# The last layer's experts: first products with their outputs on lanes, norm weight and mean folded into the second weights

## The reference, cut to what matters

```
scores = xf @ gate_w + gate_b            # expert 0 masked out, softmax, top 3
h = gelu(einsum('td,edh->eth', xf, fc1_w) + fc1_b)        # 16 experts, width 384
mu, var = h.mean(-1), h.var(-1)
h = (h - mu) * rsqrt(var + 1e-5) * ln_w[e] + ln_b[e]      # a norm inside each expert
y = einsum('eth,ehd->etd', h, fc2_w) + fc2_b
out = einsum('te,etd->td', combine, y)
```

## Time and profile before

| | us |
|---|---|
| median of 3 runs | 1077.01 (1073.15 to 1079.69) |
| profiled execution, its own time | 1074.89 |
| span of the profile | 1073.1 |
| mean granted clock | 0.876 |

### The profile page before, as it was taken

The page is one execution under the profiler, slowest core; times in us unless marked ns, Lnnn a source line. Parts: engine busy times, 40 slices in busy tenths (PEclk is TensorE's granted clock), DMA queues, the critical chain, the costliest instruction groups (busy, mean ns, idle before and its releaser), DMA issues. The chain is left out here.

```text
span 1073.1 us, 18222 instructions
## 1 busy us (share of the span) xinstructions
PE 897.4 (84%) x5969; PEld 710.9 (66%) x5969; DVE 441.0 (41%) x1153; ACT 307.6 (29%) x647; POOL 334.1 (31%) x373
## 2 busy tenths in 40 slices
PE   6887999787888887998888999998895386778684
PEld 4565899474576557777576999997665365556462
DVE  1234222322152158999482222221417926444342
ACT  2221122223344135443310222221332230323321
POOL 0002455000003218885013444443000001656650
PEclk9977899798769999999899999999986585879886
DMA  9215699100000042220043889998400004746653
GB/s 371 80 42 176 210 307 316 40 1 1 1 2 2 1 159 59 59 60 1 25 174 112 295 303 311 314 318 261 98 1 1 2 2 148 251 151 210 206 142 94
DMA packets 47378, 142.35 MB, mean 133 GB/s; under 512 B 6995, under 2 KB 11222, under 8 KB 47062
## 3 DMA queue, kind: packets, MB, share of 16 engines
q1 hardware_dynamic: 37846, 117.66, 32.3%
q0 software_dynamic: 9472, 23.93, 8.2%
HBM read 128.07 MB, written 13.50 MB: 132 GB/s over the span
## 5 line engine op out<-in xcount | busy, mean ns | idle before, releaser
L1168 POOL DMA_INDIRECT L_xr<-x_rows_L,L_rows_in x96 | 93.6, 975 | 42.2 <-issue 24.3
L1793 DVE TENSOR_TENSOR L_act<-L_hid,bank 116x512 f32<-116x512 f32 (+1 forms) x56 | 35.8, 640 | 155.8 <-ACT L_hid L1762 155.8
L1682 POOL DMA_INDIRECT y_rows_L<-L_yb,L_rows_out x56 | 55.7, 995 | 101.5 <-ACT L_yb L1768 94.9
L1762 ACT ACTIVATE L_hid<-bank 116x512 f32<-116x512 f32 (+1 forms) x56 | 31.3, 559 | 152.8 <-PE bank L1732 152.8
L1726 PE MATMUL bank<-L_xtb,L_w 128*116 128x128 f32 (+1 forms) x464 | 59.2, 282 | 0.0
L1070 POOL TENSOR_TENSOR ssm_w_low<-ssm_wbc,ssm_w_high 128x512 fp32r<-128x512 f32 x24 | 49.0, 2040 | 31.8 <-ACT ssm_w_high L1035 31.8
L1488 POOL COPY L_xrow<-L_xrow 96x384 f32<-96x384 f32 x3 | 1.5, 498 | 181.4 <-ACT L_xrow L1472 181.4
L1726 PEld LDWEIGHTS bank<-L_xtb,L_w 128*116 128x116 f32 (+1 forms) x464 | 56.6, 192 | 0.0
L1117 DVE TENSOR_TENSOR_SCAN ssm_state<-ssm_decay,ssm_drive 128x576 f32<-128x576 f32 x24 | 55.5, 2312 | 0.8
L228 PE MATMUL bank<-par_const 128*128 128x512 f32 x72 | 48.3, 800 | 0.8 <-issue 0.8
L987 PE MATMUL bank<-ssm_x_high,ssm_w_high 128*128 128x288 f32 x96 | 35.1, 365 | 13.0 <-DVE ssm_out L1122 8.8
(11 more groups left out here) (440 smaller groups left out, 2000.9 us busy)
## 6 DMA issues: line engine op xcount, KB each, us to landing
L_w<-in_L2w SPq DMA_DIRECT2D x20, 696.0 KB, 5.6
L_more<-in_L2w SPq DMA_DIRECT2D x20, 696.0 KB, 5.6
L_w<-in_L2w SPq DMA_DIRECT2D x20, 384.0 KB, 7.2
L_more<-in_L2w SPq DMA_DIRECT2D x20, 384.0 KB, 7.8
L_w<-in_L0w SPq DMA_DIRECT2D x12, 576.0 KB, 4.7
L_more<-in_L0w SPq DMA_DIRECT2D x12, 576.0 KB, 5.3
ssm_wbc<-in_wBC SPq DMA_DIRECT2D x24, 256.0 KB, 2.6
L_w<-in_L3w SPq DMA_DIRECT2D x16, 384.0 KB, 3.7
```

The lines of the kernel that those rows point to most:

```text
L1168: pool.indirect_dma_start(self.xr[j][:, :], None, self.x_rows[:, :], bass.IndirectOffsetOnAxis(ap=at, axis=0))\
L1682: pool.indirect_dma_start(X.y_rows[:, :], bass.IndirectOffsetOnAxis(ap=rows_out[h][:, j:j + 1], axis=0), y[s + j][:, :], None).then_inc(st ...
L1762: act.activation(hid[j][:, :, :], cols(gate_bank[j % 2][0:N, 0:C * R], C), ACT.Silu).then_inc(acted, 1)
L1793: dve.tensor_tensor(act_out[j][:, :, :], hid[j][:, :, :], cols(up_bank[j % 2][0:N, 0:C * R], C), ALU.mult)\
```

## The change

In the last layer's experts:

- The first product has the hidden features on the lanes (as in layers 0 and 2): 3 chunks x 2 halves, 128 tokens moving. Turning back and affine go.
- VectorE makes `centred = w2 * ln_w - shift[e]`, where `shift[e]` is the mean over the hidden features of `ln_w * w2`; this folds the norm's weight and the subtraction of the mean into the second weights. A column of ones gives the sum of the hidden values, and a one-column product with the squares their sum. The variance comes on VectorE, for two blocks at a time, its power -0.5 on GpSimd, and the output is scaled by gate x inverse deviation.
- `shift` comes from DRAM by a third load for each block, broadcast to 128 lanes. `ln_b @ w2` goes into the expert's bias (`fc2_b`).
- The steps overlap: a block's down product follows the next one's first product; SyncE loads the next step's weights after this step's first products; GpSimd's order is three gathers, the power of a pair, the fourth gather, two stores, the power of the second pair, two stores.
- Both sums over the experts' second weights, 16 x 3 products of 48 columns by 192, are made in the last attention: experts 0 to 8 between the scores and the first turned probabilities, 9 to 15 after them. There SyncE loads all second weights (288 KB each) and a selecting matrix (72 KB each), nine at a time, and ScalarE takes all scores before the first exponential.

```diff
--- head_attention
+            if also:
+                pe.wait_ge(sc_in, 7)
+                also.multiply(pe, T.bank[6], 0, 9)
             for g in range(BATCHES + 1):
                 if g < BATCHES:
                     turn(g)
+                if also and g == 0:
+                    also.multiply(pe, T.bank[6], 9, also.E)
                 if g:
                     apply(g - 1)
...
             scores(0)
             scores(1)
-            exponentials(0)
-            scores(2)
-            exponentials(1)
-            scores(3)
+            scores(2)
+            scores(3)
+            exponentials(0)
+            exponentials(1)
             take_turned(0)
             exponentials(2)
             take_turned(1)
+            also.keep_shifts(act, T.bank[6])
             add_bias(0)
...
+class SecondWeights:
+    def load(self, sp):
+        for e in range(self.E):
+            j = e % self.RING
+            if e >= self.RING:
+                sp.wait_ge(self.summed, e - self.RING + 1)
+            sp.dma_start(self.w[j][:, :], self.T.dram["L3w2"][e, :, 0:self.C * DIM]).then_inc(self.loaded[j], 16)
+            sp.dma_start(self.cols[j][:, :], self.T.dram["L3cols"][e, :, :]).then_inc(self.loaded[j], 16)
+        sp.wait_ge(self.shift_in, 1)
+        sp.dma_start(self.T.shifts, self.shift[32:48, :]).then_inc(self.stored, 16)
+        sp.wait_ge(self.stored, 16)
+    def multiply(self, pe, bank, first, end):
+        for e in range(first, end):
+            j = e % self.RING
+            pe.wait_ge(self.loaded[j], 32 * (e // self.RING) + 32)
+            for f in range(self.C):
+                mm = pe.matmul(bank[0:48, 0:DIM], self.cols[j][:, 48 * f:48 * f + 48], self.w[j][:, DIM * f:DIM * f + DIM],
+                               start=(e == 0 and f == 0), stop=(e == self.E - 1 and f == self.C - 1))
+            mm.then_inc(self.summed, 1)
...
--- run_normed_blocks, SyncE
                 for j in range(STEP):
-                    b = (q + 1) * STEP + j
-                    sp.wait_ge(down, b + 1)
-                    X.load(sp, b, STEP - s + j)
+                    sp.wait_ge(up, q * STEP + j + 1)
+                    X.load(sp, (q + 1) * STEP + j, STEP - s + j)
--- GpSimd
+                pool.tensor_copy(X.rows_in[1 - h][:, :], X.idx[:, bass.ds((q + 1) * STEP, STEP), 0]).then_inc(X.idx_in, 1)
+                pool.wait_ge(X.idx_in, q + 2)
+                fetch(0)
+                fetch(1)
+                fetch(2)
+                pool.wait_ge(stored[h], r * (16 * STEP) + 16)
+                pool.tensor_copy(rows_out[h][:, :], X.idx[:, bass.ds(q * STEP, STEP), 1]).then_inc(out_known, 1)
+                pool.wait_ge(out_known, q + 1)
+                invert(0)
+                fetch(3)
+                put(0)
+                put(1)
+                invert(1)
+                put(2)
+                put(3)
--- TensorE
+                def upwards(j):
+                    pe.wait_ge(xt_in, q * STEP + j + 1)
+                    pe.wait_ge(X.loaded[s + j], r * 48 + 48)
+                    if j >= 2:
+                        pe.wait_ge(acted, q * STEP + j - 1)
+                    for f in range(C):
+                        for c in range(2):
+                            at = I * c + N * f
+                            mm = pe.matmul(up_bank[j % 2][0:N, R * f:R * f + R], w1[s + j][:, at:at + N], xt[j][:, c, :],
+                                           start=(c == 0), stop=(c == 1))
+                    mm.then_inc(up, 1)
+                def downwards(j):
+                    pe.wait_ge(y_in, q * STEP + j + 1)
+                    pe.wait_ge(acted, q * STEP + j + 1)
+                    pe.wait_ge(weights_made, q * STEP + j + 1)
+                    for f in range(C):
+                        pe.matmul(down_bank[j][0:R, 0:DIM + 1], hid[j][:, f, :], centred[j][:, f, :],
+                                  start=(f == 0), stop=False)
+                    pe.wait_ge(squares_made, q * STEP + j + 1)
+                    for f in range(C):
+                        mm = pe.matmul(down_bank[j][0:R, DIM + 1:DIM + 2], square[j][:, f, :], p["ones"][:, 0:1],
+                                       start=False, stop=(f == C - 1))
+                    mm.then_inc(down, 1)
                 for j in range(STEP):
+                    if j + 1 < STEP:
+                        turn(pe, s + j + 1, r + 1, j + 1)
+                    upwards(j)
+                    if j:
+                        downwards(j - 1)
+                turn(pe, STEP - s, r + (2 if s else 1), STEP)
+                downwards(STEP - 1)
--- ScalarE (gelu: Gelu to hid, then Square; weigh: two outputs scaled by factor)
+                gelu(0)
+                take_gate(0)
+                take_gate(1)
+                gelu(1)
+                gelu(2)
+                take_gate(2)
+                take_gate(3)
+                gelu(3)
+                weigh(0)
+                weigh(1)
--- VectorE
+                def centre(j):
+                    dve.wait_ge(X.loaded[s + j], r * 48 + 48)
+                    dve.wait_ge(down, q * STEP + j + 1)
+                    for f in range(C):
+                        gain = C * DIM + f
+                        ins = dve.scalar_tensor_tensor(centred[j][:, f, 0:DIM], w2[s + j][:, DIM * f:DIM * f + DIM],
+                                                       w2[s + j][:, gain:gain + 1], shift[s + j][:, :], ALU.mult, ALU.subtract)
+                    ins.then_inc(weights_made, 1)
...
+                take_turned(q * STEP + 1, 1)
+                centre(0)
+                take_turned(q * STEP + 2, 2)
+                centre(1)
+                take_turned(q * STEP + 3, 3)
+                take_sums(0)
+                centre(2)
+                take_sums(1)
+                deviate(0)
+                centre(3)
+                weigh(0)
+                take_sums(2)
+                take_turned(q * STEP + STEP, STEP)
+                take_sums(3)
+                deviate(1)
+                weigh(1)
```

More of the change, by code:

```diff
@@ L1150, in __init__ @@
         self.w2 = [self.sb(f"w2_{j}", [128, self.W2]) for j in range(STEP)]
+        self.shift = [self.sb(f"shift{j}", [128, DIM]) for j in range(STEP if key == "L3" else 0)]
         self.xr = [self.sb(f"xr{j}", [R, 256 + self.E]) for j in range(SETS * STEP)]
@@ L1811, in run_normed_blocks @@
     BUFS = SETS * STEP
-    product = [T.bank[2 * j] for j in range(STEP)]
-    other = [T.bank[2 * j + 1] for j in range(STEP)]
+    up_bank, turn_bank, down_bank = (T.bank[0], T.bank[1]), (T.bank[2], T.bank[3]), T.bank[4:8]
     with ExitStack() as ctx:
@@ L1822, in run_normed_blocks @@
         X.w1, X.w2 = w1, w2
+        shift = X.shift = X.shift + sb("shiftb_", [128, DIM])
         xr = X.xr
-        xt, act_out, y = sb("xtb", [128, 2, R]), sb("act", [N, C, R]), sb("yb", [R, DIM], BUFS)
-        hid = sb("hid", [R, I])
-        total, low_mean, squares, inv = (sb(x, [R, 1]) for x in ("total", "low_mean", "squares", "inv"))
-        power = sb("power", [R, 1], 1)[0]
+        xt, hid, square, y = sb("xtb", [128, 2, R]), sb("hid", [N, C, R]), sb("square", [N, C, R]), sb("yb", [R, DIM], BUFS)
+        centred = sb("centred", [N, C, DIM + 1])
+        stat, gate_in = sb("stats", [R, 2, STEP], 1)[0], sb("gate_in", [R, STEP], 1)[0]
+        sum_sq, lifted, var, inv, factor, power = (sb(x, [R, STEP], 1)[0]
+                                                   for x in ("sum_sq", "lifted", "var", "inv", "factor", "power"))
         rows_out = [ctx.enter_context(nc.sbuf_tensor(f"{key}_rows_out{h}", [R, STEP], U32)) for h in range(SETS)]
@@ L1908, in _, with turn @@
                 pool.wait_ge(X.gathered[j], uses(n, j // STEP) * 16)
+        def turn(pe, j, times, n):
+            pe.wait_ge(X.gathered[j], times * 16)
+            for c in range(2):
+                mm = pe.transpose(turn_bank[n % 2][0:Q, R * c:R * c + R], xr[j][:, Q * c:Q * c + Q], p["ident"])
+            mm.then_inc(turned, 1)
         @block.tensor
@@ L1913, in _ @@
             pe.wait_ge(padded, STEP)
+            turn(pe, 0, 1, 0)
             def step(r, q, s):
[L1916 to L1928 removed]
@@ L1930, in turn_back @@
-                def turn_back(j):
-                    pe.wait_ge(scaled, q * STEP + j + 1)
-                    for f in range(C):
-                        mm = pe.transpose(other[j][:, R * f:R * f + R], hid[j][:, 128 * f:128 * f + 128], p["ident"])
-                    mm.then_inc(turned_back, 1)
-                def downwards(j):
-                    pe.wait_ge(hidden, q * STEP + j + 1)
-                    wd = cols(w2[s + j][0:N, 0:C * DIM], C)
-                    for f in range(C):
-                        mm = pe.matmul(product[j][0:R, 0:DIM], act_out[j][:, f, :], wd[:, f, :], start=(f == 0), stop=(f == C - 1))
-                    mm.then_inc(down, 1)
@@ L1957, in gelu @@
                     act.wait_ge(up, q * STEP + j + 1)
```

(32 more changed lines are left out.)

145 lines of the change are left out of this document (75 added, 70 removed).

## The result

The changed kernel takes 1061.76 us (median of 4, 1060.84 to 1065.36) against 1078.12 for the kernel before on the same chip (4 runs): ratio 0.9848, 95% interval 0.9814 to 0.9883. A second measurement gave 0.9843 [0.9799, 0.9887]. The forecast was 1052 us, within 1043 to 1066: the sign and the range held, the time came out 9.8 us above the forecast. The profiled execution took 1061.23 us (span 1059.4).

A forecast was written before the change was run, and what follows sets the result against it. The prediction took the last layer's expert steps to be bound by a ring through GpSimd, 14.6 us a step after the change. Profiled 1074.9 less 23.9, attention 0, gave 1051.0; half the median's 2.1 excess made 1052, range 1043 to 1066.

The forecast's parts named there:

- The ring through GpSimd, and the gathers that stood before the powers: Last layer's experts before the change: each 18.4 us step is a ring through GpSimd, four gathers (5 us) preceding the powers.
- GpSimd 14.6 us a step: GpSimd's queue per expert step after the change: 10.4 own, 1.9 powers, waits of 1.6 and 0.7, sum 14.6 us.
- rival (1): Expert steps of 15.5 to 17 us, by transfers or locks between VectorE's centring and GpSimd; 1062 to 1066 us; chance 0.20.
- Seven steps: Last layer's expert steps: second power at 933.0, six periods to 1020.6, last store ending at 1025.1; gain 23.9 us.
- TensorE 3.4 us a block: TensorE's turn, first products, down products and squares in the expert steps: 3.4 us a block, 13.6 a step without waits.
- Rival (2): Expert steps bound by TensorE at 13.6 us: gain 30, 1046 us; chance 0.10.
- Rival (4): Clock stays at 1.2 GHz in the expert steps because of one-column products: step 27.2 us, total 1139 us; chance 0.05.
- Rival (5): First Gelu behind both weighings serializes the expert steps at 17.3 us: gain 7.7, 1068 us; chance 0.06.
- The ring, 14.0: Expert steps: last down product through sums, power, weighings and Gelu 3.65 us, then first to last down product 10.3: 14.0.
- The attention hides the sums: Last attention: 96 added products fit where TensorE waits, costing 0 us, bounds -1 and +8.
- Rival (3): The last attention's clock stays cold during the added products: +8 us, 1060 us; chance 0.07.
- Transfers fit at 0.91: Expert steps' DMA transfers, including the broadcast shift: 13.3 us of each 14.6 us step, share 0.91, so they fit.

The follow-up runs named there:

- the steps alone: The new expert steps without the sums and shifts, with the attention of the kernel before: 1057.53 us, ratio 0.9788 to the kernel before.
- the run with one input: Changed kernel with the centring subtracting one column of the shift tile, so VectorE reads one tensor instead of two: ratio 0.9839 to the kernel before.
- the copies in the wait: Changed kernel with GpSimd's two copies of row numbers moved into its 1.46 us wait for the weighed rows: ratio 0.9865 to the kernel before.
- the last run: Changed kernel with row-number copies in GpSimd's wait and the next step's second block's turned rows copied before the second factors: ratio 0.9852 to the kernel before.
- the run without powers: Changed kernel with both powers of a step left out, the factor being variance times gate: ratio 0.9836 to the kernel before.

## Why the prediction was right or wrong

**The ring through GpSimd, and the gathers that stood before the powers: right.** Mean period 19.4 before (18.4 in the one step that the prediction read), 15.2 after; the steps alone give 22.9 us.

**GpSimd 14.6 us a step: measured 15.2.** The waits were over-priced, contention was left out, and part of the closeness is luck, since the two offset each other. Of the two waits (1.6 and 0.7) there is one of 1.46; the gather covers the other: -0.8. The powers take 0.72 each, not 0.65: +0.1. But two issues of each step, the first store of the second pair and the first gather, are slow: 1.75 and 1.40 us in the step shown, where their like take 0.97: +1.2. This contention was rival (1), with 0.39 for each of 12 centrings as its most. Every slow issue stands beside a centring, but not every issue beside one is slow: the gather at 994.39 takes 0.95 with three centrings running from 994.02 to 995.14. The Trainium skill (SBUF — State Buffer, "Who interferes with whom") says that a VectorE instruction with two SBUF inputs contends with a GpSimd instruction that reads SBUF. The trace agrees in that the slow issues, which take their row numbers from SBUF, stand beside the centrings, and the run with one input gave part of it back (first gathers 1.01 to 1.18 in its four middle periods). The row that the prediction set beside this rule, 0.51 us and 1.85, was of an operation with one tensor as its input beside a memset, so it didn't show this case. By the same section of the Trainium skill a `tensor_scalar` can take the shared ports in its two-port modes; that would fit the stores of 1.55 to 1.61 us left there, but no run shows that these modes were on.

**Seven steps: 110.5 forecast, 111.9 measured, from the first turn.** To the first second power 18.4 forecast, 16.3 measured (the scaled first step was too dear); six periods 87.6 against 91.2; tail 4.5 against 4.47. Two errors of 2.1 and 3.6 us partly cancel.

**TensorE 3.4 us a block: right.** Its rows of a block, down products, squares, turn, first products:

```profile
988.46 1.15 PE L2023 MATMUL bank<-L_centred,L_hid 128*128 128x193 f32 x6
989.44 0.72 PE L2027 MATMUL bank<-par_const,L_square 128*128 128x1 f32 x6
990.03 0.40 PE L1996 MATMUL bank<-par_const,L_xr 128*96 128x128 f32 x2
990.27 1.50 PE L2014 MATMUL bank<-L_xtb,L_w 128*128 128x128 f32 x12
```

From start to start 0.98 for the down products (forecast 1.08), 0.59 for the squares (0.68), 0.24 for the turn and 1.34 for the first products, until the next down products start at 991.61 (forecast 0.22 and 1.43): 3.2 us. Rival (2), 13.6 us a step, was not reached: GpSimd was slower, and in the variants that relieve it 13.7 to 13.9 came only twice. Rival (4), a clock at 1.2 GHz through the steps, did not come about: one-column products leave it at 1.00. Something like it is real on a small scale: single steps in which the clock falls took 1.7 us more; that one-column products have a part in it isn't shown. Rival (5) failed: no step waits for a Gelu behind both weighings. What TensorE does wait for at a step's start is VectorE's turned copy behind the second factor, 0.5 to 1.4 us.

**The ring, 14.0: too short, as far as the variants show it.** Once GpSimd's queue has slack, it waits for the variances and TensorE for the turned copy, and the periods at clock 1.00 are 14.8 to 16.0 us (the run with one input, and the copies in the wait). So this bound, or another that the last run leaves open, stood closer behind GpSimd's queue than the prediction had it.

**Centring 0.39 us: measured 0.411**, and hidden on VectorE; what it costs is on GpSimd, as said.

**The attention hides the sums: right, to the microsecond.**

```profile
833.05 11.32 PE L771 MATMUL bank<-sw_w,sw_cols 128*48 128x192 f32 x54 [0.49 <-ACT a_att_sc L641]
844.20 1.70 PE L595 MATMUL bank<-par_const,a_att_sc 108*64 108x108 f32 x32
845.69 6.99 PE L771 MATMUL bank<-sw_w,sw_cols 128*48 128x192 f32 x42
853.34 1.75 PE L595 MATMUL bank<-par_const,a_att_sc 108*64 108x108 f32 x32 [0.66 <-DVE a_att_sc L726]
```

Less the 7.4 to 7.5 us by which this profile stands later, the first 54 run from 825.5 to 836.8 (forecast 825.5 to 836.6), the others until 845.2 (846 to 847), and the attention takes 73.4 us instead of 73.3. Rival (3) failed. What the step "the bias product has its old shape: 0" missed is behind it: the norm and routing meet another clock, some 3 us in the comparison with the two variants that lack this part, 1.0 against the profile of before. Why is not shown.

**Transfers fit at 0.91: right** (0.80 to 0.94 by step), and the margin is thin: a step of 13.89 us in the run without powers has them at 0.99.

**The sum.** The weakest steps are its base, 1074.9 plus 1, and the attention's 0. The 9.8 us by which the sum fell short are made up so. 2.2 are the base: from the median of its own chip, 1078.12 less 23.9 is 1054.2. The profiled execution was 3 to 7 us faster than the medians of before measured since (1078 to 1082), and only 1 of this had been added. 1.4 are the stage. 3.5 (0.3 to 6.6) are the attention's part. The last 2.7 no run explains; they are within the intervals (steps alone less attention's part make 19.4, and 16.4 was measured, 12.6 to 20.1).

## What to carry to other kernels

When a ring is cut, work out the queue of the engine that issues the gathers as a sum of its own issues, and add to every gather its landing time, here 2.8 to 5.5 us where TensorE was waiting for it, before moving it: each of four reorderings of this ring gave back as much elsewhere, or more. Take a gain off the median of several executions and not off the one that was profiled, which here was 3 to 7 us fast. Ask of any change what it does to TensorE's granted clock in the stages behind it too, and don't judge a difference of 3 us in a stage from one profile each.

## What the runs showed of the hardware that was not expected

- GpSimd's issue of an indirect transfer mostly takes 0.95 to 1.04 us. In the last five periods 10 of 40 take 1.36 to 1.80, all beside a centring on VectorE that reads two tensors from SBUF; the third gather of each of these steps takes 0.95 beside one. With one tensor some still take 1.55 to 1.61.
- The granted clock fell in single steps (0.80 over 17.06 us) of a kernel that held 1.00 in all of them in another execution, with the same instructions.
- Over 22 executions of the kernel before, 0.01 of mean granted clock went with 9.6 us of 1080.
- With work added beside an attention, the granted clock of the norm behind it was another: 1.00 or 0.58 over the same 4 us behind the projection, also with 80 of the 96 added products taken out again. The kernel before itself, in its one profile, lies between.
- Where TensorE waited for a gather of 128 rows, it could turn them 2.8 to 5.5 us after the gather's issue had ended (the changed kernel and the two that move the fourth gather).
